# Token layout for the next group made a group ahead, in four parts, in a fused decoder layer

## The reference, cut to what matters

```python
# x, ctx: (16, 128, 256) fp32; self-attention 16 heads of 64, cross-attention 16 heads of 16
x = x + attn(layernorm(x), W_Q, W_K, W_V, W_O)          # each sequence of 128 tokens by itself
x = x + xattn(layernorm(x), ctx, ctx, mask, Wq, ...)    # keys and values from the context
x = x + ffn(layernorm(x))                               # 8 experts of 512, top-1 gate, dense sum

def attn(x, ...):
    Q, K, V = (einsum('btd,hkd->bthk', x, W) + b for W, b in ...)
    a = softmax(einsum('bqhk,bshk->bhqs', Q, K) / 8)
    return einsum('bqhk,hdk->bqd', einsum('bhqs,bshk->bqhk', a, V), W_O) + b_O
```

## Time and profile before

| What | Value |
|---|---|
| Median of 3 runs | 931.63 us |
| Profiled execution | 930.06 us, of which span 928.3 us |
| PE busy | 870.9 us (94%) |
| ACT, DVE, POOL busy | 629.4, 561.7, 309.3 us |
| Mean granted TensorE clock | 0.986 of full |

### The profile page before, as it was taken

The page is one execution under the profiler, slowest core; times in us unless marked ns, Lnnn a source line. Parts: engine busy times, 40 slices in busy tenths (PEclk is TensorE's granted clock), DMA queues, the critical chain, the costliest instruction groups (busy, mean ns, idle before and its releaser), DMA issues.

```text
span 928.3 us, 18067 instructions
## 1 busy us (share of the span) xinstructions
PE 870.9 (94%) x6299; PEld 786.1 (85%) x6299; DVE 561.7 (61%) x1159; ACT 629.4 (68%) x1764; POOL 309.3 (33%) x355
## 2 busy tenths in 40 slices
PE   8898999999899987999998879999999999999997
PEld 7697888889888876788878869999999999999996
DVE  5787888788878865777878754454223422342223
ACT  4886887788788764898989856764454445444543
POOL 5554564555445567564746530000000000000000
PEclk9999999999999998899999999999999999999999
DMA  5410000000000007655637013320000000000000
GB/s 185 137 35 1 1 2 1 2 24 1 1 1 2 1 1 182 127 155 100 168 81 186 9 47 101 95 77 24 0 0 0 23 0 0 0 23 1 1 1 23
DMA packets 21787, 42.21 MB, mean 45 GB/s; under 512 B 3144, under 2 KB 3152, under 8 KB 21712
## 3 DMA queue, kind: packets, MB, share of 16 engines
q1 hardware_dynamic: 21120, 40.91, 16.2%
q10 hardware_dynamic: 592, 0.34, 0.2%
HBM read 30.75 MB, written 10.49 MB: 44 GB/s over the span
## 4 chain that ended last, share of the span: by engine, by line
PE 63%; DVE 16%; ACT 13%; issue 4%; DMA 2%; POOL 1%; SPq 1%; DVEq 0%; ACTq 0%; POOLq 0%
PE Y L529 23%; PE A L529 19%; PE S L529 12%; ACT probs L862 7%; DVE PT L939 3%; PE T L630 3%; DVE nm L1035 2%; DVE arena L1004 2%; PE O L529 2%; DVE oraw L1054 2%; PE O L647 1%; DVE arena L939 1%; ACT PT L870 1%; ACT opart L876 1%; DVE XT L973 1%
## 5 line engine op out<-in xcount | busy, mean ns | idle before, releaser
L939 DVE TENSOR_TENSOR PT<-probs,PT 128x512 fp32r<-128x512 f32 x128 | 89.6, 700 | 230.9 <-ACT PT L919 230.9
L529 PE MATMUL A<-XT,arena 128*128 128x512 f32 x804 | 213.5, 400 | 4.1 <-DVE arena L1004 3.0
L862 ACT ACTIVATE probs<-S,nm 128x128 f32<-128x128 f32 x512 | 181.0, 370 | 43.9 <-DVE nm L1035 42.3
L529 PEld LDWEIGHTS Y<-arena,PT 128*128 128x128 f32 x1536 | 200.3, 191 | 11.0 <-DVE PT L939 1.1
L529 PE MATMUL Y<-arena,PT 128*128 128x256 f32 x1536 | 204.1, 283 | 0.3
L1267 POOL TENSOR_TENSOR probs<-probs,rinv 128x512 f32<-128x512 f32 x128 | 133.3, 1041 | 175.1 <-DVE rinv L1040 175.1
L529 PEld LDWEIGHTS A<-XT,arena 128*128 128x128 f32 x804 | 142.1, 190 | 33.8 <-DVE arena L1004 9.6
L919 ACT ACTIVATE PT<-probs 128x512 fp32r<-128x512 f32 x128 | 80.8, 631 | 90.9 <-PE Y L529 90.5
L862 ACT ACTIVATION_READ_ACCUMULATOR probs<-S,nm 128x1 f32 x512 | 107.3, 210 | 0.0
L939 DVE TENSOR_TENSOR PT<-T,PT 128x512 fp32r<-128x512 f32 x128 | 87.5, 684 | 24.9 <-ACT PT L870 23.0
L529 PE MATMUL S<-XT,arena 128*128 128x512 f32 x390 | 100.3, 394 | 0.0
(11 more groups left out here) (123 smaller groups left out, 1325.8 us busy)
## 6 DMA issues: line engine op xcount, KB each, us to landing
wst<-in_pieces SPq DMA_DIRECT2D x52, 256.0 KB, 2.6
stage<-arena SPq DMA_DIRECT2D x32, 256.0 KB, 2.4
arena<-stage SPq DMA_DIRECT2D x48, 128.0 KB, 4.3
arena<-stage SPq DMA_DIRECT2D x24, 256.0 KB, 3.8
xs<-in_x SPq DMA_DIRECT2D x4, 512.0 KB, 4.5
craw<-in_ctxT SPq DMA_DIRECT2D x4, 512.0 KB, 4.5
out<-craw SPq DMA_DIRECT2D x4, 512.0 KB, 2.6
rowc<-in_rows ACTq DMA_DIRECT2D x1, 264.0 KB, 5.9
```

The costliest lines, as they stand in the source:

```text
L529: mm = pe.matmul(acc, lhs[a], rhs[b], start=first and i == 0, stop=last and i == 2, skip_group_check=shared)
L862: last = act.activation(probs[:, n % 4, u * P:(u + 1) * P], S[n % 2][:, u * P:(u + 1) * P], ACT.Exp, bias=nm[:, n % 4, u:u + 1], accum_out ...
L939: dve.tensor_tensor(out_, src, hi.bitcast(F32), ALU.subtract).then_inc(sem_, 1)
```

## The change

- A second token buffer: group 0 and 2 of self-attention use `CT[0]` (the context's first buffer), groups 1 and 3 `XT`, and group 0 of cross-attention `XA`, the place of two weight pieces that are no longer needed.
- For groups 1 to 3 of self-attention and group 0 of cross-attention ("parted"), statistics move to slots 10 and 11 of the group before (two tiles each), aggregation to slot 12, normalisation to slots 13 and 14 (two tiles each).
- Their transposition is done in four parts (`transpose_part`): two tiles of one feature half each, 128x256, into columns 256 to 511 of bank A1, the half that the V job doesn't use. Part i stands before V job 11 + i, so in slots 15, 0, 1 and 2, and is written back in the next slot (`part_hi`, `part_lo`). Part i waits for the low half of V job 10 + i and of part i - 1; its copy waits for V job 11 + i; V job 15 waits for the fourth part's subtraction.
- V and Q/K job 15 are written back one slot later, as all others.
- The first context is split in slots 5 to 8 of group 3, after the Q/K and V jobs of group 2; the zeroing of the region where `XA` lies waits for the third cross Q/K job.

```diff
+        XA = arena[:, 8192:10240].rearrange("p (s k t) -> p s k t", s=2, k=KD)
+        NORM_PARTED = {-3: ALL[:2], -2: ALL[2:]}
+        PARTS_AT = -1
+        def parted(ph, g):
+            return ph == 0 and not opening(g) or ph == 1 and opening(g)
+        def tokens_t(ph, g):
+            if ph == 0:
+                return XT if g % 2 else CT[0]
+            return XA if ph == 1 and opening(g) else XT
...
-            if name in ("qk_out", "v_out", "qk_last", "v_last"):
-                own = name.endswith("last")
-                done = [j for j, halves in steps(name.split("_")[0], ph, g, v if own else v - 1)
-                        if 1 in halves]
-                return [(j,) for j in done if own == (ph == 0 and j == 15)]
+            if name in ("qk_out", "v_out"):
+                return [(j,) for j, halves in steps(name.split("_")[0], ph, g, v - 1) if 1 in halves]
...
+            if name in ("xp", "xp_out"):
+                part = v - PARTS_AT - (name == "xp_out")
+                return [(part,)] if parted(ph, g) and 0 <= part < 4 else []
+            if parted(ph, g) and name in ("stats", "norm", "aggr"):
+                tiles = {"stats": STATS1[1], "norm": NORM_PARTED, "aggr": {AGGR1[1]: None}}[name]
+                return [] if v not in tiles else [()] if name == "aggr" else [(tiles[v],)]
+            if parted(ph, g) and name[:2] == "xt":
+                return []
...
-            run(order, does, 0, 0, ())
+            run(order, does, 0, 0, (), later=((0, 1),))
             for g in range(1, GROUPS):
-                run(order, does, 0, g, ((0, g - 1),))
+                run(order, does, 0, g, ((0, g - 1),),
+                    later=((0, g + 1) if g + 1 < GROUPS else (1, 0),))
...
         PE_ORDER = (
-            (("scores", "quad", (0, 0)), ("xt1", "xt1", (0, 0)), ("proj", "proj", (4, 6)),
-             ("pv", "quad", (2, 5)), ("transpose", "quad", (1, 3)), ("v", "v", (0, 0)),
-             ("qk", "qk", (0, 0)), ("xt0", "xt0", (0, 0))),
+            (("scores", "quad", (0, 0)), ("proj", "proj", (4, 6)),
+             ("pv", "quad", (2, 5)), ("transpose", "quad", (1, 3)), ("xp", "xp", (0, 0)),
+             ("v", "v", (0, 0)), ("qk", "qk", (0, 0))),
...
         ACT_ORDER = (
-            (("probs", "quad", (2, 4)), ("xt1", "xt1_out", (0, 0)), ("v", "v_out", (0, 0)),
-             ("qk", "qk_out", (0, 0)), ("exp", "quad", (0, 1)), ("out", "quad", (2, 5)),
-             ("v", "v_last", (0, 0)), ("qk", "qk_last", (0, 0)), ("xt0", "xt0_out", (0, 0))),
+            (("probs", "quad", (2, 4)), ("xp", "xp_out", (0, 0)), ("v", "v_out", (0, 0)),
+             ("qk", "qk_out", (0, 0)), ("exp", "quad", (0, 1)), ("out", "quad", (2, 5))),
...
-             ("xt1", "xt1_out", (0, 0)), ("max", "quad", (0, 0)), ("residual", "residual", (4, 6)),
-             ("v", "v_out", (0, 0)), ("qk", "qk_out", (0, 0)), ("stats", "stats", (0, 0)),
-             ("aggr", "aggr", (0, 0)), ("norm", "norm", (0, 0)), ("v", "v_last", (0, 0)),
-             ("qk", "qk_last", (0, 0)), ("xt0", "xt0_out", (0, 0))),
+             ("max", "quad", (0, 0)), ("residual", "residual", (4, 6)),
+             ("v", "v_out", (0, 0)), ("xp", "xp_out", (0, 0)), ("qk", "qk_out", (0, 0)), ("stats", "stats", (0, 0)),
+             ("aggr", "aggr", (0, 0)), ("norm", "norm", (0, 0))),
...
                     if job == 0:
-                        pe.wait_ge(xt_lo, nth(XTE, ph, g, KD - 1))
+                        tokens_done(ph, g, KD - 1)
+                    if job == 15:
+                        pe.wait_ge(xp_lo, xpe(0, g + 1, 3))
...
+            def transpose_part(ph, g, i):
+                pe.wait_ge(ln_x, nth(GRP, ph, g, 0))
+                pe.wait_ge(v_lo, nth(VJ_F1, 0, g - 1 if ph == 0 else GROUPS - 1, 10 + i))
+                pe.wait_ge(xp_lo, xpe(ph, g, i - 1))
+                for j in range(2):
+                    t, k = i // 2 * 2 + j, i % 2
+                    mm = pe.transpose(A1[:, D + j * P:D + (j + 1) * P], xn[:, t, k * P:(k + 1) * P],
+                                      ident[:, :])
+                mm.then_inc(xp_ps, 1)
...
+            def part_hi(ph, g, i):
+                cols, k = slice(i // 2 * D, i // 2 * D + D), i % 2
+                act.wait_ge(xp_ps, xpe(ph, g, i))
+                act.wait_ge(v_ps, nth(VJ, 0, g - 1 if ph == 0 else GROUPS - 1, 11 + i))
+                if ph == 0 and g >= 2:
+                    act.wait_ge(qk_ps, nth(QK, 0, g - 2, 15))
+                    act.wait_ge(v_ps, nth(VJ, 0, g - 2, 15))
+                if ph == 1:
+                    act.wait_ge(qk_ps, nth(QK, 0, GROUPS - 1, 11))
+                act.activation(tokens_t(ph, g)[:, 0, k, cols], A1[:, D:2 * D], ACT.Copy).then_inc(xp_hi, 1)
...
+            def part_lo(ph, g, i):
+                cols, k, to = slice(i // 2 * D, i // 2 * D + D), i % 2, tokens_t(ph, g)
+                dve.wait_ge(xp_hi, xpe(ph, g, i))
+                sub_lo(to[:, 1, k, cols], A1[:, D:2 * D], to[:, 0, k, cols], xp_lo)
...
+                    if to == 0:
+                        pool.wait_ge(qk_ps, nth(QK, 0, GROUPS - 2, 15))
+                        pool.wait_ge(v_ps, nth(VJ, 0, GROUPS - 2, 15))
...
+                    if n == 8:
+                        pool.wait_ge(qk_ps, nth(QK, 1, g, 2))
...
-                    if g == 2 and 4 <= n < 8:
-                        split_context(0, g, 0, n - 4)
+                    if g == GROUPS - 1 and 5 <= n < 9:
+                        split_context(0, g, 0, n - 5)
```

More of the change, by code:

```diff
@@ L75, with xte, xpe @@
 MSTEP_F4 = Count(4, (0, 0, MCH))
-XTE = Count(0, (KD, KD, KD))
+def xte(ph, g, k):
+    return (g if ph == 1 else g + GROUPS if ph == 2 else 0) * KD + k + 1
+def xpe(ph, g, i):
+    return (g - 1 if ph == 0 else GROUPS - 1) * 4 + i + 1
 LNST = Count(0, (TILES, TILES, TILES))
@@ L212, in build @@
         v_lo = sem("v_lo")
+        xp_ps = sem("xp_ps")
+        xp_hi = sem("xp_hi")
+        xp_lo = sem("xp_lo")
         xt_ps = sem("xt_ps")
@@ L531, in three, with tokens_done @@
                 return mm
+            def tokens_done(ph, g, k):
+                if parted(ph, g):
+                    pe.wait_ge(xp_lo, xpe(ph, g, 3))
+                else:
+                    pe.wait_ge(xt_lo, xte(ph, g, k))
             def bank_free(g, i):
@@ L537, in bank_free @@
                     pe.wait_ge(v_lo, nth(VJ_F1, 1, g - 1, g == 1))
-                elif i < 2 or (g > 0 and i == 2):
-                    pe.wait_ge(xt_lo, nth(XTE, 1, g, i - (g > 0)))
+                elif g == 0 and i == 0:
+                    pe.wait_ge(v_lo, nth(VJ_F1, 0, GROUPS - 1, 15))
+                    pe.wait_ge(xp_lo, xpe(1, g, 3))
+                elif g == 0 and i == 1:
+                    pe.wait_ge(qk_lo, nth(QK_F1, 0, GROUPS - 1, 15))
+                elif g > 0 and i < 3:
+                    pe.wait_ge(xt_lo, xte(1, g, i - 1))
                 else:
@@ L546, in project_qk @@
                     c, is_k = job // 2, (job + 1) % 2
-                    i, col, src, bank = 4 * (c // 2) + is_k, (c % 2) * P, XT, bank_qk(ph, g, job)
+                    i, col, src, bank = 4 * (c // 2) + is_k, (c % 2) * P, tokens_t(ph, g), bank_qk(ph, g, job)
                     if not (opening(g) and job in (0, 1, 3)):
@@ L552, in project_qk @@
                             keep_busy(5)
-                        pe.wait_ge(xt_lo, nth(XTE, ph, g, KD - 1))
+                        tokens_done(ph, g, KD - 1)
                 else:
                     c, is_k = CROSS[job]
-                    i, col, src, bank = N1 + is_k, c * P, CT[g % 2] if is_k else XT, bank1(g, job)
+                    i, col, src, bank = N1 + is_k, c * P, CT[g % 2] if is_k else tokens_t(1, g), bank1(g, job)
                     if 0 in halves:
@@ L561, in project_qk @@
                     else:
-                        pe.wait_ge(xt_lo, nth(XTE, 1, g, halves[-1]))
+                        tokens_done(1, g, halves[-1])
                 weight_ready(pe, w_order(i) - 1)
@@ L576, in project_v @@
                     if job == 0:
-                        pe.wait_ge(xt_lo, nth(XTE, ph, g, KD - 1))
-                    i, src, bank = 4 * (job // 4) + 2, XT, bank_v(g, job)
+                        tokens_done(ph, g, KD - 1)
+                    if job == 15:
+                        pe.wait_ge(xp_lo, xpe(0, g + 1, 3))
+                    i, src, bank = 4 * (job // 4) + 2, tokens_t(ph, g), bank_v(g, job)
                     tiles = [(job % 4, 0)]
@@ L728, in _ @@
                 "qk": project_qk, "v": project_v,
+                "xp": transpose_part,
                 "xt0": lambda ph, g: transpose_group(ph, g, 0),
@@ L735, in up @@
                 if m == 0:
-                    pe.wait_ge(xt_lo, nth(XTE, 2, g, KD - 1))
+                    pe.wait_ge(xt_lo, xte(2, g, KD - 1))
                 pe.wait_ge(e_split, m + 1)
@@ L798, in tokens_hi @@
                 for k in halves:
-                    act.wait_ge(xt_ps, nth(XTE, ph, g, k))
```

(22 more changed lines are left out.)

1 line of the change is left out of this document (added).

## The result

The changed kernel takes 915.36 us (median of 4 runs, 914.49 to 915.75) against 931.23 before (4 runs): ratio 0.9835, 95% interval 0.9819 to 0.9851. The forecast was 917.4. Five more runs of it beside the last experiments gave a median of 915.38. Its profiled execution has a span of 912.7 us, 15.6 less than before. Small differences need care. One slot that the change doesn't touch, slot 8 of group 0, took 6.76 us here at a mean granted clock of 0.75, and 8.34 at 0.60 in a later profile of the same kernel (run 12).

The account below looks back on a forecast made before the run. TensorE, busy 94% of the span, was taken to bound the kernel, so only its waits at group boundaries could be gained. -20.8 + 4.6 + 1.2 + 0.4 + 0.4 = -14.2 from 931.6 gave 917.4 us, range 914 to 923.

Parts of the forecast that it names:

- Removed excess, 20.8: Four group boundaries of self-attention: each loses its excess over steady slots, 5.04 to 5.64 us, in sum 20.8 us.
- The four parts, 20.08 per boundary: Slots 0 to 3 at 4.82 or 5.22 us each, plus 0.1 in slot 15: 1.16 us added per boundary, 4.6 for four.
- Just in time: Shared bank: the part's subtraction ends at about 136.0, TensorE comes there at 136.19 less semaphore delay, so cost 0.
- The moved layer norm, 1.2 in all: Slots 10 to 14 of the group before: layer norm work there costs 0.3 us per group, 1.2 for four.
- Group 0, 0.4: Slot 12 of group 0: POOL's power holds up the weight split, costing 0.4 us, bounds 0 and 1.3.
- Rival 3: Port collisions: each of the eight norm pieces loses 0.6 us, 4.8 in all, giving 922.2 us; chance 0.03.
- Slots 4 and 5, 0.4: Slot 4 behind the boundaries now has a write-back: 0.14 us times 3, 0.4 added; nothing at the last boundary.
- The last boundary: Start of cross-attention: TensorE's order times the DMA queue's first copy, so all moves earlier, the copy by some 14 us.
- rival 2: Last boundary gives nothing because a DMA or memset times cross-attention's start: 4.2 us lost, 921.6 us; chance 0.06.
- The sum: Whole kernel: -20.8 + 4.6 + 1.2 + 0.4 + 0.4 = -14.2 us.
- Rival 4: VectorE fills slots 10 to 3, so its added work counts in full: no gain, 931 us; chance 0.07.
- Rival 5: Shared bank's round trip exposed, 1.4 us per part: slower, 935 us; costs more than it brings from about 1.15; chance 0.07.

Follow-up runs that it names:

- run 12: The changed kernel itself, unmodified, measured again beside the last experiments: 915.38 us.
- run 1: The kernel before, with the layer norm alone moved a group ahead and tokens still transposed whole in slots 3 and 4: 924.79 us.
- Runs 2 to 4: Changed kernel with an extra VectorE read of the part in slots 1 and 3, in slots 0 and 2, or transpositions doubled: 917.67, 917.91, 916.58 us.
- run 3: The changed kernel with one extra VectorE read ahead of the part's subtraction in slots 0 and 2: 917.91 us.
- run 5: The changed kernel with the part's subtraction behind that of Q or K in VectorE's order: 927.40 us.
- runs 8 to 10: The changed kernel with cross Q, K and V jobs a slot earlier, POOL's zeroing moved to idle slots, or both: 914.62, 914.32, 913.65 us.
- Run 2: The changed kernel with one extra VectorE read ahead of the part's subtraction in slots 1 and 3: 917.67 us.
- run 6: The changed kernel with parts of groups 1 to 3 transposed in every other slot, layer norm two slots further ahead: 912.96 us.

## Why the prediction was right

- **Removed excess, 20.8.** Right. All four boundaries lost it, and run 1 shows that it was two stalls, in the places named.
- **The four parts, 20.08 per boundary.** Right to 0.1: measured 20.07 to 20.18. So were the single slots: forecast 4.82 and 5.22, measured 4.84, 5.24, 4.85, 5.23. Runs 2 to 4 show the two reasons given, TensorE's in slots 0 and 2, K's subtraction in 1 and 3. "Just in time" for the bank's round trip was right too, with some 0.1 us to spare (run 3); run 5 shows what is behind it.
- **The moved layer norm, 1.2 in all.** Too high. In groups 1 and 2 slots 11 to 15 grew by nothing: 4.95, 4.54, 4.95, 4.56, 4.90 add up to 23.90, before 23.91. A slot that is 0.06 longer is followed by one that is as much shorter. My reading is that TensorE, which has no more work than before, takes back in the next slot what it waited; no run isolates this. The slot with a weight subtraction, from which I took the 0.14, was slot 5, with TensorE busy for 4.48 of 4.89: not a slot of TensorE's, so a poor model for slots 11 to 15.
- **Group 0, 0.4.** The size was near (0.56 in slot 13), by luck, for the reason was wrong. My own step had POOL's weight split held up behind the power; I then argued that normalisations "stand right before the reciprocal for which POOL's next normalise waits, so POOL is idle there". That fails just where the split has been held up into that place. Rival 3, given 0.03, did happen, once instead of eight times.
- **Slots 4 and 5, 0.4.** Right in groups 2 and 3: 9.51 after, 9.37 before. In group 1 these slots were no shorter before, so the sum is 0.3.
- **The last boundary.** Right that all of it moves: the DMA queue's first copy goes from 348.37 to 332.18. That is 16.2 earlier, more than the 14 forecast, and the first normalise of cross-attention goes with it, from 370.94 to 354.82; so rival 2 fell. The chain comes through the DMA queue as forecast. What I didn't see is how near POOL's queue stood behind it: 0.17 us (runs 8 to 10).
- **The sum** was -14.2; the profiled spans differ by 15.6, the medians by 15.9. From the one to the other: layer norm and group 0 cost 0.6 instead of 1.6, slot 15 nothing instead of 0.4, the boundaries 0.2 more than forecast, and the clock gave a net 0.2. Before, the slot at 341.88 had a granted clock of 0.67 and took 5.11 us; after, its counterpart has 1.00 and takes 4.49:

```profile
326.32:330.81 4.49, 4.17 (x30) 3.71 (x30) 2.43 (x6) 3.28 (x11) 2.17 (x3) 1.00 0.00 0
```

A slot early in cross-attention went from 3.72 to 3.05 in the same manner (granted clock 0.82 and 1.00), and 1.1 us were given back around the start of the experts. These are low stretches that fall elsewhere, which I had put at 1 to 2 us in either sign.
- **Rival 4** (VectorE fills the slots) is excluded by the time, by slots 11 to 15, which took 2.1 us more of VectorE's work and grew by nothing, and by VectorE's busy share at the boundaries, 16.85 of 20.16. Run 2 doesn't speak against it: in slots 1 and 3, whose end VectorE's order sets, added work does count in full.
- **Rival 5** (round trip exposed) is what run 5 built. By the rival's own count, which takes the transposition in, a part costs (23.24 - 19.02) / 4 = 1.06 us there, under the 1.15 from which I had it cost more than it brings, and the run is faster than the kernel before. The crossing point itself was not tried.

## What to carry to other kernels

In a software pipeline across engines, ask of each slot which engine's order sets its end, and put half-steps of added work where the other engine does: the same transposition and write-back cost 1.1 us per group in one placement and nothing in another. An operation between two others on a second engine is priced by what it pushes back, not by its own time: swapping two neighbours was worth 12 us. And before earlier work is bought, look through the whole queue of the engine that comes next, not only at the wait that shows.

## What the hardware showed beyond expectation

A pair of VectorE normalisations of 128x256 from and to SBUF takes 0.73 us alone, 1.25 and 1.75 where the first of the two has most of a POOL instruction to wait out, and 0.92 where little is left of it (run 6, at 129.44). Of the 40 single normalisations in the changed kernel's trace nine took 0.50 to 1.23 us instead of 0.41, and each of them ended 0.15 us behind the end of a POOL instruction. The loss shows as a longer instruction, not as idle time, so no view of waits lists it. Four 128x128 transpositions take 0.63 us busy but 0.39 of TensorE's time, two cost 0.22 in a full queue. The clock: all profiled kernels have some stretch at half clock (1.2 GHz) around the start of cross-attention. In the two main ones the first such stretch there follows one in which TensorE was busy for little over half of the time (2.34 of 4.48 us before, 5.25 of 9.00 between 343 and 352 after), but place and length of such stretches differ between kernels of equal work there. Another lies in slot 8 of group 0, behind a wait of TensorE of 3.3 us, and differs even between two executions of one kernel (6.76 us at a granted clock of 0.75, 8.34 at 0.60). What decides these was not tried.
